# Feed-forward groups of four tiles inside the attention steps, one pipeline over all 192 tiles

## What is computed

```python
for i in range(DEPTH):                       # DEPTH = 6
    x = attn_layer(shift_tokens(x), Wqkv[i], q_scale[i], k_scale[i], Wo[i]) + x
    x = ffn_layer(shift_tokens(x), ln_g[i], ln_b[i], W1[i], b1[i], W2[i], b2[i]) + x
# attn_layer: q, k of 16 heads of 64, each divided by its norm, rotated by tables;
#   a window of 32 queries sees its own 32 keys and the 32 before; softmax; output times Wo
# ffn_layer: xn = layernorm(x) * g + b;  (a, gate) = split(xn @ W1 + b1)  (341 each)
#   return a * gelu(gate) @ W2 + b2
# shift_tokens: the second half of the channels comes from the token before
```

## Time and profile before

| | |
|---|---|
| median of 3 runs | 3574.35 us (3574.1 to 3577.07) |
| profiled execution, own time | 3575.57 us |
| its span, first to last instruction | 3573.7 us |
| busy share of the span | TensorE 91%, its weight loads 62%, VectorE 78%, ScalarE 82%, GpSimd 57% |
| mean granted TensorE clock | 0.958 of 2.4 GHz |
| DMA | 57.58 MB, mean 16 GB/s |

### The profile page before, as it was taken

How to read it: one execution, slowest core, us unless ns; L and a number is a source line. 1 busy time by engine, 2 the same in 40 slices (tenths; PEclk the granted TensorE clock), 3 DMA queues, 4 the chain that set the end, 5 groups by cost and what they waited for, 6 DMA issues and landing times. The chain is left out here.

```text
span 3573.7 us, 118257 instructions
## 1 busy us (share of the span) xinstructions
PE 3252.6 (91%) x42076; PEld 2208.0 (62%) x42076; DVE 2791.6 (78%) x5370; ACT 2933.6 (82%) x9257; POOL 2045.7 (57%) x2150
## 2 busy tenths in 40 slices
PE   5699998889999789999789999978999977999977
PEld 4466665656666556666566666665666655666656
DVE  7788887578888568888658888757888856888865
ACT  3399998479999459999649999937999955999973
POOL 3566665456666356666446666545666634666644
PEclk8799999899999899999899999989999989999999
DMA  2000001100000100000110000010000010000011
GB/s 70 10 7 8 7 7 33 22 13 7 7 7 6 47 15 8 7 7 7 37 24 7 8 7 7 10 44 14 7 8 7 6 43 19 8 7 7 7 34 42
DMA packets 141061, 57.58 MB, mean 16 GB/s; under 512 B 118598, under 2 KB 137668, under 8 KB 139460
## 3 DMA queue, kind: packets, MB, share of 16 engines
q1 hardware_dynamic: 140484, 50.01, 5.9%
HBM read 22.57 MB, written 2.10 MB: 7 GB/s over the span
## 5 line engine op out<-in xcount | busy, mean ns | idle before, releaser
L1321 ACT ACTIVATE probs<-s_ps,nbias,rnorm 128x64 f32<-128x64 f32 x3072 | 1229.9, 447 | 1.6 <-DVE nbias L1039 0.9
L1524 POOL TENSOR_TENSOR qk_rot<-by_cos,by_sin 128x1024 f32<-128x1024 f32 x384 | 914.0, 2380 | 381.9 <-DVE by_sin L989 334.8
L597 PE MATMUL ring<-wvo,xsT 128*32 128x512 f32 x6144 | 794.8, 600 | 10.2 <-ACT vo L1144 10.2
L1321 ACT ACTIVATION_READ_ACCUMULATOR probs<-s_ps,nbias,rnorm 128x1 f32 x3072 | 765.0, 249 | 0.0
L1513 POOL TENSOR_TENSOR probs<-probs,rrow 128x256 f32<-128x256 f32 x768 | 454.6, 613 | 429.1 <-DVE rrow L973 429.1
L986 DVE TENSOR_TENSOR by_cos<-qk_ps,rotary 128x1024 f32<-128x1024 f32 x378 | 463.0, 1225 | 147.1 <-ACT squares L1307 147.1
L1533 POOL TENSOR_TENSOR qk_rot<-qk_rot,rnorm 128x1024 f32<-128x1024 f32 x192 | 365.5, 1904 | 341.4 <-DVE rnorm L733 341.4
L543 PEld LDWEIGHTS ring<-cst,qk_rot 128*128 128x128 f32 x3072 | 341.3, 141 | 243.7 <-ACT vo L1144 155.9
L543 PE MATMUL ring<-cst,qk_rot 128*128 128x128 f32 x3072 | 446.4, 278 | 27.6 <-POOL qk_rot L1524 24.4
L1001 DVE TENSOR_REDUCE sumsq<-squares 128x16 f32<-128x1024 f32 x384 | 462.9, 1206 | 0.0
L989 DVE TENSOR_TENSOR by_sin<-qk_ps,rotary 128x1024 f32<-128x1024 f32 x378 | 459.2, 1215 | 0.0
(11 more groups left out here) (166 smaller groups left out, 5433.4 us busy)
## 6 DMA issues: line engine op xcount, KB each, us to landing
qk_rot<-L_ffn_Wqkv SPq DMA_DIRECT2D x7, 1024.0 KB, 5.1
xs<-x_tok SPq DMA_DIRECT2D x194, 32.0 KB
xs<-x_tok SPq DMA_DIRECT2D x194, 31.8 KB
by_cos<-x_tok SPq DMA_DIRECT2D x48, 128.0 KB
by_cos<-x_tok SPq DMA_DIRECT2D x48, 127.0 KB
wv<-L_ffn_Wqkv SPq DMA_DIRECT2D x7, 512.0 KB, 6.6
wo_pad<-L_ffn_Wo SPq DMA_DIRECT2D x14, 256.0 KB, 7.3
xs<-x_tok SPq DMA_DIRECT2D x194, 0.2 KB
```

Of the source, the lines that this page charges most:

```text
L597: last = mm(r[WIN * mh:WIN * (mh + 1), :], xsT[:, a, WIN * w:WIN * (w + 1)], wvo[:, mh, :, :], start=True, stop=True)
L1321: last = nc.scalar.activation(probs[:, a, h // 4, :, h % 4, :], s_ps[:, half, c:c + 2 * WIN].rearrange("p (s c) -> p s c", s=2), ACT.Exp, ...
L1524: g.tensor_tensor(qk_rot[:, n, :], by_cos[:, n, :], by_sin[:, n, :], ALU.add).then_inc(added[qk], 1)
```

## The change

The loops over layers go. Every engine runs one unrolled `step(k)` for k = 0 to 201 over 192 tiles (32 of each layer in turn). Feed-forward group U (four tiles) is done inside the steps k = 6 + f + 4U: tokens of three tiles loaded at f = 0 and of the fourth at f = 1, centring and deviation at f = 1 (its squares on GpSimd, in step f = 0 of that engine, which runs about a step behind VectorE), Newton operations at f = 2, normalising and transposes at f = 3, all six products by W1, the gelus and the hidden products at f = 4, down and the new x at f = 6. So of four steps in turn one has f = 0 and 4, one f = 1, one f = 2 and 6, one f = 3.

The products of the group go through the ring of four banks instead of banks of their own. The layer norm's scale goes into W1 (ScalarE and VectorE, step 8 of a layer) and its bias through a small product into b1. W1's parts, the next layer's q and k weights and a second `wvo` get room of their own; the room comes from `x_keep`, which is written to the output at the start and loaded again, four tiles at a time, for the last additions on GpSimd. Weights are loaded at steps 4, 7, 9 and 12 of a layer, `wvT` and `wvo` of the next layer computed at steps 13 to 23, the split of q's and k's weights at step 31, the rotary tables in eight parts at steps 24 to 31. The output leaves group by group. Semaphore values and addresses, formerly computed in registers from the layer number, are constants. The waits of 471 and 642 become waits on the tiles and weights concerned. The core of the diff:

```diff
+TILES = DEPTH * NT
+GROUPS = DEPTH * NG
+LAST_RESIDUAL = FT - 1 + 3
+STEPS = LAST_RESIDUAL + FT * (GROUPS - 1) + 8
...
+        def group(k, f):
+            u, rest = divmod(k - LAST_RESIDUAL - f, FT)
+            return u if rest == 0 and 0 <= u < GROUPS else None
...
+        NEXT_VALUES = (("wvT0", 13), ("wvT1", 15), ("wvo0", 17), ("wvo1", 19), ("wvo2", 21), ("wvo3", 23))
+        def ring_uses(k):
+            tile_uses = [[("xsT", k), ("qT0", k - 1), ("vo3", k - 2), ("vo1", k - 1), ("o", k - 3), ("vo2", k - 1),
+                          ("vo0", k - 1), ("kT0", k - 1)],
+                         [("qT1", k - 1), ("kT1", k - 1), ("pT0", k - 2), ("pT1", k - 2)]]
+            before, after = [[(use, T) for use, T in part if 0 <= T < TILES] for part in tile_uses]
+            first = [("b1", layer_at(k, 8))]
+            ups = [(f"gate{i}", group(k, 4)) for i in range(3)] + [(f"up{i}", group(k, 4)) for i in range(2)]
+            ups += [(part, next_layer_at(k, at_step)) for part, at_step in NEXT_VALUES]
+            last = [("up2", group(k, 4)), ("xn", group(k, 3)), ("down", group(k, 6))]
...
+            return first + before + ups + after + last
...
@@ tensor: the order of a step @@
+                bias_product(layer_at(k, 8))
+                xs_transposed(0)
+                transposed("q", 0, 1)
+                scores(1, 2)
+                values(3, 2)
+                project("q", 0, 0)
+                project("q", 1, 0)
+                values(1, 1)
+                output(3)
+                values(2, 1)
+                values(0, 1)
+                transposed("k", 0, 1)
+                for i in range(3):
+                    up("gate", i, group(k, 4))
+                project("k", 0, 0)
+                project("k", 1, 0)
+                up("up", 0, group(k, 4))
+                up("up", 1, group(k, 4))
+                for part, at_step in NEXT_VALUES:
+                    next_values(next_layer_at(k, at_step), part)
+                transposed("q", 1, 1)
+                transposed("k", 1, 1)
+                scores(0, 1)
+                probs_transposed(0, 2)
+                probs_transposed(1, 2)
+                up("up", 2, group(k, 4))
+                normalised_transposed(group(k, 3))
+                down(group(k, 6))
...
@@ vector: the order of a step @@
+                xsT_lower(0)
+                sum_of_squares("k", 1)
+                maxima(1, 2)
+                lower(group(k, 4))
+                centre(group(k, 1))
+                biases(layer_at(k, 8))
+                inverse_norms(0, 1, 1)
+                softmax_bias(1, 2)
+                inverse_norms(1, 6, 1)
+                row_reciprocals(0, 2)
+                inverse_norms(6, RSQRT_OPS, 1)
+                rotate("q", 0, 0)
+                rotate("q", 1, 0)
+                group_deviation(group(k, 1))
+                vo_evacuated(2, 1)
+                residual(3)
+                normalised(group(k, 3))
+                row_reciprocals(1, 2)
+                k_evacuated("low", 0, 1)
+                w1_lower(layer_at(k, 8))
+                sum_of_squares("q", 0)
+                hidden(0, group(k, 4))
+                hidden(1, group(k, 4))
+                rotate("k", 0, 0)
+                maxima(0, 1)
+                rotate("k", 1, 0)
+                x_new(group(k, 6))
+                softmax_bias(0, 1)
+                hidden(2, group(k, 4))
...
@@ scalar: the order of a step @@
+                xsT_upper(0)
+                q_evacuated(0, 1)
+                exponentials(0, 2)
+                normalised_upper(group(k, 4))
+                w1_upper(layer_at(k, 8))
+                exponentials(2, 2)
+                exponentials(4, 2)
+                xsT_evacuated(0)
+                exponentials(6, 2)
+                square("q", 0)
+                next_wqk_upper(next_layer_at(k, NT - 1), 0)
+                exponentials(8, 2)
+                exponentials(10, 2)
+                vo_evacuated(3, 2)
+                vo_evacuated(1, 1)
+                exponentials(12, 2)
+                exponentials(14, 2)
+                k_evacuated("high", 0, 1)
+                vo_evacuated(0, 1)
+                gelu(group(k, 4))
+                square("k", 0)
+                next_wqk_upper(next_layer_at(k, NT - 1), 1)
...
@@ gpsimd: the order of a step @@
+                next_wqk_lower(next_layer_at(k, NT - 1), 0)
+                add_rotated("q", 0)
+                group_rsqrt(group(k, 2))
+                add_rotated("k", 0)
+                normalise_k(0)
+                squared4(group(k, 0))
+                next_wqk_lower(next_layer_at(k, NT - 1), 1)
+                normalise(0, 1)
+                x_and_bias(group(k, 3))
+                normalise(1, 1)
+                for j in range(TPB):
+                    next_table(next_layer_at(k, NT - TPB + j + 1), j)
...
@@ sync: a step @@
+                if k + 2 < TILES:
+                    attention_tokens(k + 2)
...
+                U = group(k, 0)
+                if U is not None:
+                    ffn_first_rows(U, 0, 1).then_inc(g_edge, 16)
+                    ffn_tokens(U, 0, FT - 1)
+                    ffn_first_rows(U, 1, FT - 1).then_inc(g_xs, 16)
+                U = group(k, 1)
+                if U is not None:
+                    ffn_tokens(U, FT - 1, FT)
+                    ffn_first_rows(U, FT - 1, FT).then_inc(g_xs, 16)
...
+                U = group(k, 7)
+                if U is not None and U >= GROUPS - NG:
+                    sp.wait_ge(x_ready, NT + FT * (U + 1))
+                    sp.dma_start(out4[U % NG], x_cols(U % NG * FT, FT)).then_inc(out_done, 16)
```

More of the change, by code:

```diff
@@ L289, in heads, with layer_at, next_layer_at, wvo @@
             return ap.rearrange("p (h d) -> p h d", h=n)
[L295 to L302, removed]
+        def group(k, f):
+            u, rest = divmod(k - LAST_RESIDUAL - f, FT)
+            return u if rest == 0 and 0 <= u < GROUPS else None
+        def layer_at(k, step, first=0):
+            l, rest = divmod(k - step, NT)
+            return l if rest == 0 and first <= l < DEPTH else None
+        def next_layer_at(k, step):
+            l = layer_at(k, step)
+            return l + 1 if l is not None and l + 1 < DEPTH else None
+        def wvo(l):
+            return wvo_odd if l % 2 else wvo_even
+        NEXT_VALUES = (("wvT0", 13), ("wvT1", 15), ("wvo0", 17), ("wvo1", 19), ("wvo2", 21), ("wvo3", 23))
[8 more added lines that the diff above has]
+            last = [("up2", group(k, 4)), ("xn", group(k, 3)), ("down", group(k, 6))]
+            first, ups, last = [[(use, n) for use, n in part if n is not None] for part in (first, ups, last)]
+            return first + before + ups + after + last
+        ring_bank, uses = {}, 0
+        for k in range(STEPS):
+            for use in ring_uses(k):
+                ring_bank[use] = uses % RING_BANKS
+                uses += 1
         def schedule(loop, step, depth, n, after_loop=None):
@@ L316, in schedule, with every_step, there @@
                 step(k, k % 2, None)
[L318 to L322, removed]
+        def every_step(step):
+            for k in range(STEPS):
                 step(k)
-        def tile_numbers(l, k):
-            return k, NT * l + k
-        def there(k, it, s, n=NT):
+        def there(k, it, s, n=TILES):
             return it is not None or 0 <= k - s < n
@@ L1119, in _ @@
-                every_tile(step, 3, before_last=lambda: normalised(0, 0))
-                dve.wait_ge(b1_in, 96 * l + 96)
-                normalised(1, 1)
-                lower(0, 0)
-                lower(1, 1)
-                centre(2, 0)
-                variance4(2, 0)
-                hidden(0, 0, 0)
-                with dve.Fori(0, (NG - 4) // 2) as it:
-                    for par in range(2):
-                        step4(2 * it + par, par, True, True, True)
-                for u in range(NG - 4, NG):
-                    step4(u, u % 2, u + 1 < NG, u + 2 < NG, u + 3 < NG)
@@ L1425, in _ @@
+            every_step(step)
         @block.gpsimd
@@ L1491, in first_weights @@
                 pool.wait_ge(rotary_in, 16)
-                tables(0)
+                pool.wait_ge(sc_in, 32)
+                for j in range(TPB):
+                    table(0, j).then_inc(tables_ready, 1)
                 for part in range(2):
```

1392 lines of the change are left out of this document (657 added, 735 removed).

## The result

The changed kernel took 3582.64 us (median of 16 runs) beside 3574.8 before (16 runs): a ratio of 1.0022, 95% interval 1.0014 to 1.003, so slower by 0.2%. The record said 3566, inside a range of 3415 to 3690, and leaned to faster (0.50 to 0.42). The sign was wrong.

What follows compares the result with a forecast made beforehand. Attention was taken as bound by TensorE and ScalarE hand in hand, engines waiting in order, 14.05 us a tile. 2827.4 + 616 (46 groups of 13.4) + 60 - 19 + 80 = 3564.8 span, forecast 3566 us, range 3415 to 3690.

Steps and rivals of the forecast that it cites:

- A, +5.1: Step with a group's gates and ups: 5.1 us longer than 14.05, from TensorE's 18 products, gelus and table load.
- B, +4.9: Centring step: 4.9 us longer, mostly because VectorE's centring waits for the fourth tile's token load until 6.6.
- C, +3.0: Step with down products: 3.0 us longer, 2.68 for down plus 0.3 left from B; Newton falls into GpSimd's waits.
- D, +0.4: Normalising step: 0.4 us longer for four transposes; VectorE's and GpSimd's additions lie in waits.
- Constants, -19: Register waits and addresses become constants throughout: 0.1 us a tile gained, 19 us in all.
- Layer changes, 12 each: Next layer's weights, rotary tables, wvo, wvT and bias products add 12 us at each change, 60 in all.
- Tail, 80: After the last tile's start: drain with C and A work 43 us, then an uncovered chain 33 and 4 more.
- Some wait I missed: Rival: an unforeseen wait, such as bank order, makes the kernel slower; chance 0.04.
- The load does not hold VectorE: Rival in B: fourth tile's load lands in time, B adds only 1.7, 147 us less, 3419; chance 0.22.
- TensorE and ScalarE drift apart: Rival: the two engines separate further, extras overlap, 9 us a group, 3364; chance 0.05.
- The table switch costs more than its row: Rival: ScalarE held 1.4 us more in each of 92 switches, 127 us, 3693; chance 0.04.
- The clock falls in B: Rival: TensorE's 3.1 us wait for vo's bank halves its clock, 2.5 us a group, 115, 3681; chance 0.15.

Runs made afterwards that it cites:

- e5: Changed kernel with GpSimd's addition of rotated k made by four 128x256 instructions instead of one: 3531.8 us, ratio 0.9882 to the kernel before.
- e4: Changed kernel with gelu left out, the gates going through Identity, so no table loads for it: 3586.1 us, ratio 1.003 to the kernel before.
- e10: Changed kernel with load, Newton, bias, deviation and q-weight work reordered, plus a tiny exponential behind k's square in A to load its table early: 3307.1 us.
- e3: Changed kernel with the group's fourth-tile loads issued first in SP's step B, ahead of the transpose wait and attention loads: 3426.1 us, ratio 0.9582.
- e7: Changed kernel with fourth-tile load earlier, Newton behind k's addition, softmax bias ahead of x_new, and gates through Identity: 3346.5 us, against 3372.6 with gelu.
- e8: Changed kernel with fourth-tile load earlier, Newton behind k's addition, bias ahead of x_new, and deviation moved from B to C: 3365.5 us, against 3372.6 without that.

## Why the prediction was right or wrong

**The step that failed** is this one, in C: "GpSimd's twelve small Newton operations, 3.3 by 0.28 each, fall into its waits ... and what is left over does not reach TensorE's down products." I asked only who waits for Newton, not what Newton pushes where. It pushed a 2.37 us addition onto an instruction of 0.16 us for which ScalarE waits. Its price is the collision, 7.6 us a layer (567.5, the mean of the second to fifth layer of the changed kernel, less 559.9 in e5), 46 in all; the medians give 51. I had such an effect in the upper end for B ("VectorE's small operations of B held up by GpSimd's two probability products") and not where it occurred.

The other terms, by e5, which is the changed kernel without the collision of C and D; in its last layer, without layer-change work, the four steps take 18.8, 18.4, 17.1 and 14.3:
- **A, +5.1**: 4.8 measured. TensorE bounds it, so ScalarE's load and gelus cost nothing there (e4, e10: A unmoved).
- **B, +4.9**: 4.4 to 5.0. The load let the centring start 6.5 to 8.0 into the step, 6.75 in the median of 46 B, 6.6 forecast, and its share was 3.25, 3.2 forecast (e3). What stood behind it was mis-named: the table load above all, not the centring and the deviation (e7, e8).
- **C, +3.0**: 3.05. **D, +0.4**: 0.25 without the collision.
- **Constants, -19**: not seen. Steps 2 to 6 of the first layer, which hold attention alone, take 14.1, 14.5, 13.9, 14.1 and 13.9, mean 14.11; the same five steps of the kernel before take 14.15 in each of its layers. So it is 0.04 a tile, 8 us over 192 tiles, at most.
- **Layer changes, 12 each**: 559.9 - 8 x 68.6 = 11.
- **Tail, 80**: 3581.2 - 3504.6 = 76.6. The first tile 150.3, for 148.4; over the traces of the runs it lies between 145.9 and 151.6, though the front is the same in all.

Without the collision four steps were to take 69.6 - 0.4 = 69.2 and took 68.6: 46 x 0.6 = 28 less. 3564.8 - 28 + 46 - 3 + 2 = 3582, and the span is 3581.2 (one us less for each layer change is left out). So the nearness to the median is in part luck: an overestimate of A and B paid for more than half of what was missed, and the sign hung on the rest. What the forecast said of the whole (what the barrier cost is paid back in each group) is what the trace shows: a layer takes 567.5, forecast 568.8, 570.0 before.

**The rivals.** *Some wait I missed*, slower, at 0.04, is the one that came true: the wait for the held bias. *The load does not hold VectorE* was false of the kernel, and its price right: 147 us forecast, 157 measured once e3 made it true. *TensorE and ScalarE drift apart* did not come: a group costs 68.6 - 4 x 14.05 = 12.4 more than bare attention without the collision, not 9. *The table switch costs more than its row*: no; each load is 1.28 with nothing behind it, as before.

*The clock falls in B* came true in most B (it was also named as a sign that the forecast is wrong), and cost nothing that shows. In 33 of 46 B the granted clock fell below 1.00 behind TensorE's wait for the copy of `vo`; these waits were 2.17 to 3.72 us, most near 2.44, and 29 of the 33 under 3.1, which I had taken to lie between; that it takes a wait of some 3.5 us was wrong. Two B with a wait of 2.43, in one the clock falls and in the other not (stretches of four us, the first from 0.4 us before the end of the wait; then TensorE's later wait in the second B; PEclk is third from the end):

```profile
1744.00:1748.00 4.00, 3.43 (x15) 2.06 (x16) 3.12 (x5) 3.29 (x12) 3.92 (x4) 0.64 0.00 0
1748.00:1752.00 4.00, 4.00 (x59) 3.08 (x58) 4.00 (x8) 2.94 (x5) 2.87 (x4) 0.94 0.02 4
2879.30:2883.30 4.00, 3.09 (x18) 1.59 (x18) 3.12 (x5) 3.58 (x12) 3.89 (x4) 1.00 0.00 0
2883.30:2887.30 4.00, 3.03 (x56) 2.58 (x57) 4.00 (x8) 2.69 (x4) 2.90 (x4) 1.00 0.02 4
```

```profile
2884.27 1.09 PE L581 MATMUL ring<-cst,qk_rot 128*128 128x128 f32 x8 [1.06 <-DVE x_tok L1062]
```

Both steps take 18.4. Where the clock holds, TensorE waits 1.06 us for the residual; where it falls, the products at 1.2 GHz fill that wait. I had 1.5 us of such cover and 2.5 uncovered; the clock came back within some four us in 32 of the 33, and the loss was covered. The mean B with a fallen clock is longer (19.2 beside 18.6), but so is the work at those places of a layer: at the same place and with the same wait the two kinds agree (the fifth B of a layer 19.3 with and without, the seventh 18.4 with and without). For waits over 2.7 there is no B with a held clock to compare with.

e3 shows the price without cover. 40 of its B have a wait of 0.91, and the clock held in all. Five, the last B of a layer, have one of 1.86, and in two of them the clock fell (four us from the end of the wait, where it held and where it fell):

```profile
652.00:656.00 4.00, 4.00 (x27) 2.56 (x27) 3.65 (x8) 3.95 (x12) 2.46 (x5) 1.00 0.00 0
1193.10:1197.10 4.00, 3.96 (x18) 2.65 (x19) 3.71 (x8) 3.21 (x11) 2.46 (x5) 0.67 0.00 0
```

The two take 17.7, the other three 16.2: 1.5 us in the step. The next step makes it good (18.3 behind the two, 19.8 to 21.0 behind the others), so that even this does not reach the total.

## What to carry to other kernels

When work is inserted into an in-order queue, ask what it pushes, and onto which instruction of which other engine it falls; a tiny instruction on the critical path is the one to check against long ones of an engine that can hold it, as GpSimd held VectorE here, and an order that avoids it cost nothing here. A late load is first a question of its place in the issuing queue. A cost that is hidden is hidden by something: remove that and measure it again, since taking the table loads out was worth nothing in the changed kernel and 26 us with the other moves, and moving one of the two into a wait was worth 45. The version with all moves (e10) beats both kernels: 3307.1, 7.5% under the kernel before.

## What the runs showed of the hardware that I had not expected

- A VectorE instruction of 128x8 with two inputs in SBUF takes 1.89 us beside a GpSimd addition of 128x1024 that began before it, and 0.24 to 0.77 where the addition is cut in four, whose pieces take 0.71 to 0.77 each: it is held only until the running one ends.
- An instruction with a single input in SBUF was held too. In the changed kernel this one (VectorE) lies beside the addition that began at 851.11 and ends at 853.50; where nothing holds it, it takes 0.17. What that costs the kernel was not measured.

```profile
852.48 1.07 DVE L1032 TENSOR_SCALAR sumsq<-sumsq 128x32 f32<-128x32 f32 x1
```

- TensorE's granted clock fell after waits of 2.17 us and up in some steps of the changed kernel (in e3 after one of 1.86), and held through waits up to 2.67 in others; the wait's length alone does not say which. The Trainium skill (TensorE: Matmul & The Clock Gate, Why this matters for your kernels) asks for no idle gaps over about 3 us between bursts of products; in the changed kernel the clock fell 25 times behind shorter ones.
- Four additions of 128x256 on GpSimd take 2.80 us for 2.37 in one piece: 0.14 us more for each cut.
